# Attention on one Trainium2 core: TensorE takes the scores of two steps, then the P times V products of two earlier steps, by turns

## The reference

```python
x = x + _L0_conv_ref(_gn(x), w_qkv, w_proj, b_proj)          # attention over the 1024 pixels, 8 heads of 48
x = x + _L1_conv_ref(_gn(x), proj_w, proj_b, off_w, off_b, mask_w, mask_b, gamma, beta)   # deformable 3x3 convolution, batch norm, GELU
```

```python
attn = jnp.einsum('bhnd,bhmd->bhnm', q, k) * SCALE
attn = jax.nn.softmax(attn, axis=-1)
out = jnp.einsum('bhnm,bhmd->bhnd', attn, v)
```

## Time and profile before

| | |
|---|---|
| time before, median of 3 runs | 3718.53 us (3712.7 to 3722.61) |
| the profiled execution | 3713.13 us, its span 3711.2 us |
| TensorE matmuls busy | 3324.8 us (90%) |
| VectorE, ScalarE, GpSimd busy | 2285.5 (62%), 1694.9 (46%), 1278.6 us (34%) |
| TensorE clock granted, mean | 0.96 of full |
| the attention stage, batch 1 | 652.88 us to about 757 us |

### The profile page before, as it was taken

One profiled execution on the slowest core, in us unless ns is written; L12 is line 12 of the kernel. 1 busy time (PEld: TensorE's weight loads), 2 busy tenths in 40 slices (PEclk: granted clock), 3 DMA queues, 4 the chain that ended last, 5 costly groups with the idle time before them and its releaser, 6 DMA issues.

```text
span 3711.2 us, 88927 instructions
## 1 busy us (share of the span) xinstructions
PE 3324.8 (90%) x33434; PEld 1912.5 (52%) x33434; DVE 2285.5 (62%) x3746; ACT 1694.9 (46%) x2708; POOL 1278.6 (34%) x1183
## 2 busy tenths in 40 slices
PE   4799899989999899998999899998999989997991
PEld 1245555545555455554555455564555545554660
DVE  5576566755767567665676557675676756764343
ACT  3155443644436444454436444374444544454443
POOL 0043232622326133342335233271333523353440
PEclk8689999999999999999999999999999999998996
DMA  3000000100010000100001000100001000001007
GB/s 132 0 19 36 1 2 3 37 35 2 2 37 3 35 2 2 37 36 1 2 2 38 35 1 2 37 3 35 2 1 37 19 18 1 2 20 69 1 1 306
DMA packets 12151, 97.80 MB, mean 26 GB/s; under 512 B 2777, under 2 KB 2905, under 8 KB 4972
## 3 DMA queue, kind: packets, MB, share of 16 engines
q1 hardware_dynamic: 9468, 67.41, 4.7%
q0 software_dynamic: 1152, 12.58, 0.8%
q10 hardware_dynamic: 1008, 11.01, 0.8%
HBM read 56.26 MB, written 34.60 MB: 24 GB/s over the span
## 4 chain that ended last, share of the span: by engine, by line
PE 51%; issue 23%; POOL 15%; DVE 5%; ACT 4%; DMA 1%; DVEq 0%; POOLq 0%; SPq 0%; ACTq 0%
PE R L1513 20%; POOL PL L612 13%; PE R L1494 12%; PE G L1258 6%; PE G L1291 5%; PE G L1482 2%; DVE MXP L1010 2%; PE R L1406 2%; PE R L1331 1%; DVE M L1187 1%; ACT PL L849 1%; PE G L1474 1%; PE G L1433 1%; PE G L1428 1%; ACT P L786 1%
## 5 line engine op out<-in xcount | busy, mean ns | idle before, releaser
L1513 PE MATMUL R<-P,WALL 128*128 128x512 f16 x3888 | 980.5, 379 | 0.3 <-issue 0.3
L1010 DVE TENSOR_REDUCE MXP<-G 128x1 f32<-128x512 f32 x1024 | 693.7, 688 | 173.8 <-PE G L1291 165.8
L612 POOL TENSOR_TENSOR PL<-P 128x1024 f16<-128x1024 f32 x256 | 574.3, 2248 | 626.8 <-ACT P L769 624.7
L1494 PE MATMUL R<-MHL,XB 128*128 128x240 f16 (+14 forms) x7776 | 720.3, 235 | 2.5 <-DVE P L1208 2.5
L649 POOL TENSOR_TENSOR MHL<-M,MHL 128x280 f16<-128x280 f32 (+2 forms) x576 | 364.8, 636 | 852.7 <-ACT MHL L859 851.5
L769 ACT ACTIVATE P<-R 128x1024 f32<-128x1024 f32 x512 | 521.2, 1024 | 237.7 <-PE R L1331 230.9
L1494 PEld LDWEIGHTS R<-MHL,XB 128*128 128x128 f16 x7776 | 569.9, 98 | 103.7 <-DVE P L1208 2.8
L1513 PEld LDWEIGHTS R<-P,WALL 128*128 128x128 f16 x3888 | 378.7, 98 | 395.1 <-issue 0.5
L1060 DVE TENSOR_TENSOR PL<-P 128x1024 f16<-128x1024 f32 x256 | 453.4, 1771 | 175.7 <-ACT P L769 175.5
L1331 PE MATMUL R<-QK 48*128 48x512 f16 (+1 forms) x3072 | 437.0, 393 | 53.2 <-issue 33.7
L1291 PE MATMUL G<-QK,QZ 112*128 112x512 f16 x1024 | 411.4, 403 | 45.2 <-DVE MXP L1010 17.1
(11 more groups left out here) (127 smaller groups left out, 3315.3 us busy)
## 6 DMA issues: line engine op xcount, KB each, us to landing
XA<-x SPq DMA_DIRECT2D x8, 1536.0 KB, 9.0
X<-x SPq DMA_DIRECT2D x8, 1536.0 KB, 6.5
x_scratch<-X SPq DMA_DIRECT2D x7, 1536.0 KB, 5.1
y_scratch<-XP ACTq DMA_DIRECT2D x7, 1536.0 KB, 7.6
WALL<-y_scratch SPq DMA_DIRECT2D x6, 1536.0 KB, 14.8
out<-WALL POOLq DMA_DIRECT2D x6, 1536.0 KB, 11.0
QK<-x_scratch SPq DMA_DIRECT2D x4, 1536.0 KB, 17.7
P<-wd SPq DMA_DIRECT2D x9, 576.0 KB, 4.7
```

The lines of the kernel that those rows point to most:

```text
L612: pool.tensor_tensor(PL[:, s % P_BUFS, :], P32[:, s % P_BUFS, :], high_view(s), ALU.subtract).then_inc(p_low_pool, 1)
L1010: dve.reduce_max(MXP[:, name[1] % 2, n // 2, n % 2:n % 2 + 1], chunk(sec, name)[:, :], AX.X).then_inc(dve_read, 1)
L1494: last = pe.matmul(out, XT[:, x_part, g * BOX_Y + r, t * 128:(t + 1) * 128], MHL[:, m_part, o + at:o + at + (hi - lo) * (x1 - x0)], start= ...
L1513: last = pe.matmul(R6[:, CT + ct, :], WALL[:, w:w + 128], PHL[:, u % 2, part // 2, t, :], start=(u % TAPS == 0 and n < CT), stop=(u % TAPS ...
```

## The change

TensorE's loop goes over two steps at a time. It issues both scores, then all that both steps had between them, then the two products that are 3 and 2 steps behind the even step. No instruction is added or removed, and the other engines' programs, their waits, the buffers and `LAG` stay as they are.

```diff
-                for s in range(STEPS + LAG):
+                for s in range(0, STEPS + LAG, 2):
                     if s < STEPS:
                         scores(s)
-                        for name in step_chunks(s, not final):
+                        scores(s + 1)
+                        for name in step_chunks(s, not final) + step_chunks(s + 1, not final):
                             if name[0] == "gn":
                                 group_mean(name, sec, b * 2 + 2)
                             else:
                                 fill_chunk(name, sec, b)
                     elif not final:
-                        fill_chunk(DRAIN[s - STEPS], sec, b + 1)
-                    if s >= LAG:
-                        pv(s - LAG)
+                        for name in DRAIN[s - STEPS:min(s - STEPS + 2, LAG)]:
+                            fill_chunk(name, sec, b + 1)
+                    for k in (s - LAG, s - LAG + 1):
+                        if 0 <= k < STEPS:
+                            pv(k)
                 if not final:
                     fill_chunk(DRAIN[LAG], sec, b + 1)
```

## The result

The changed kernel takes 3726.2 us (median of 14 runs, 3723.3 to 3730.2), the one before beside it 3716.45 (14 runs). The ratio is 1.0026, with a 95% interval of 1.0017 to 1.0034: slower by a quarter of a per cent, 9.8 us. Forecast was 3699, faster. The time lies in the stated range, but the direction is the wrong one. The profiled execution took 3723.3 us, 10.2 more than the one before.

What follows compares the result with a forecast made beforehand. TensorE's order of matmuls was taken as the bound. Seven batches at 6.3 - 3.3 - 1.0 = 2.0 and a last at 6.3 - 0.9 - 0.2 = 5.2 make 19.2 us less: 3699 from the median, range 3684 to 3737.

Steps and rivals of the forecast that it cites:

- The order: TensorE's two-step round: fewer changes between scores and pv make 2.93 into 2.72, saving 0.21, 6.3 us a batch.
- the loop: Odd exponential, its wait for pv(s - 3), scores and pv: 2.66 a round, 0.06 below 2.72, so not binding.
- the rival that made it the bound: Odd exponential's wait for pv(s - 3) longer than 0.83 makes ScalarE's loop the bound: slower, up to 3743; chance 0.14.
- The insertion: Two ScalarE operations between exponentials after steps 24, 32 and 40: 1.71 lost each time, in seven batches.
- the group mean: Group mean's share in the cost of ScalarE's other work: 0.23 a batch, in seven batches.
- the pair of low parts: VectorE's and GpSimd's low parts wait for each other: 2.84 a pair, falling behind by 0.12 a round.
- low part 20: Late at step 20, where VectorE waits for GpSimd's power behind low part 19: 0.9 of waiting, 1.0 a batch in all.
- Block normalising, o_norm and the readings: 0: These wait for things done over a microsecond earlier, so they cost 0.
- last batch, drift of the pair relieved by step 38: Low parts fall behind for 17 rounds x 0.12 less 1.1: 0.9 by step 38, where transposes relieve it.
- the first: Rival: VectorE and GpSimd's low parts set every round at 2.84; 3719, chance 0.15.
- The second and third: Rivals: ScalarE's loop becomes the bound, up to 3743, chance 0.14; change of shape isn't the cost, 3737, chance 0.08.
- The case "better": Nothing late on the low parts' side: 3.0 a batch, last 6.1, 3691; insertions also no dearer, 3669; chance 0.14.

Runs made afterwards that it cites:

- e12: e7 with 6 added matmuls nobody reads between the two scores in rounds 26, 34 and 42 of the first seven batches; single run, 3702.4 us.
- e7: Changed kernel with GpSimd's low part cut to 128 of 1024 columns, the rest of odd steps' low part left out; 3699.7 us, 0.9956.
- e2: Changed kernel with the transpose of step 61 moved to step 62; 3715.7 us, ratio 0.9989 to the kernel before.
- e10: Changed kernel with 6 added matmuls nobody reads between the two scores in rounds 26, 34 and 42 of the first seven batches; 3741.65 us, 1.0064.
- e3: Changed kernel with rounds 26, 34 and 42 of the first seven batches in TensorE's old order; 3711.8 us, 0.9987.
- e4: Changed kernel with the edits of e1, e2 and e3 together; 3705.5 us, ratio 0.9966 to the kernel before.
- e11: Changed kernel with ScalarE's insertions moved behind the exponentials of steps 25, 33 and 41; 3714.1 us, 0.9992.
- e6: Changed kernel with GpSimd's power ahead of low part 19, transpose at 62, old order in rounds 18, 20, 22, 26, 34, 42 except last batch; 3693.7 us, 0.9941.
- e1: Changed kernel with VectorE's group-norm shift (L975) ahead of the low part of step 22 instead of step 20; 3727.4 us, 1.0028.
- e5: Changed kernel with GpSimd's group-norm power computed ahead of low part 19 instead of behind it; 3708.5 us, 0.9983.
- e8: Kernel before with GpSimd's low part cut to 128 of 1024 columns, the rest of odd steps' low part left out; 3710.5 us, 0.9984.

## Why the prediction was wrong, point by point

**Right.** The order: six more scores at once, the shape changes saved, a round of 2.72. ScalarE's odd exponential waits for pv(s - 3), 0.87 behind its start where 0.83 was taken, and the loop doesn't bind: the rival that made it the bound needed 0.15 more than 0.83. The insertion costs 4.45 - 2.72 = 1.73 where 1.71 was worked out, the group mean 0.22 for 0.23. That the turns between scores and pv are the cost, and not a semaphore each, stands on the same 2.72. Whether it is the rows of the tiles or another thing in which the two differ (their types, their columns) was not tried. With low parts and falls away the whole working is there: 89.65 - 86.68 = 2.97 a batch (e12, forecast 3.0) and 6.14 in the last (forecast 6.1). And the pair of low parts at 2.84, which the last batch shows in 12 of its rounds.

**Wrong, with sizes.** From 19.2 faster to 10.2 slower, by the profiled executions, are 29.4 us (by the medians 29.0):

| step of the prediction | forecast | shown | us in all |
|---|---|---|---|
| the granted clock, in no term of the sum | 0 | falls in the stage 14.4, in the first five steps 2.6 | 17.0 |
| low part 20, "0.9 of waiting there" (1.0 a batch) | 1.0 | 6.79 - 4.46 (e7) = 2.33 | 9.3 |
| "Block normalising, o_norm and the readings: 0" | 0 | 0.72, 0.90 in the last | 5.9 |
| last batch, drift of the pair relieved by step 38 | 0.9 | 82.71 (e2) - 81.23 (e7) = 1.5 | 0.6 |
| all else, the most of it between the stages | | | -3.4 |

- *The clock.* The sum was made at the granted clock of 1.00 that the earlier trace rows shows, and costed each stall at its own length. The stalls that the change makes are followed by stretches at half clock. Counted from the intervals they cost 1.4 in the two rounds from step 33 in six of seven batches (8.5), 1.0 in three behind step 20 (3.1) and 1.4 twice in the first batch (2.8). e10, e12, e3, e4, e11 and e6 have none from step 33. From 700 us on in batch 1, TensorE's longest wait for an exponential is 0.2 us in e10 and e12, 0.9 in e3, e4 and e6, and 1.0 in e11: no fall from step 33 on in any of these six kernels' 42 batches. It is 1.6 in the changed kernel, e1, e2 and e5, and falls from step 33 on stand in 7, 7, 7 and 3 of their seven batches. e12 against e7 gives 17.6 for the falls in a kernel without low parts. The clock is the largest term and decided the sign: without its 17.0 the changed kernel would be 6.8 faster.
- *Low part 20.* The prediction named the queue behind the power, and gave L975, which is 0.16 in the earlier trace rows, no price of its own. L975 has two inputs in SBUF, and GpSimd's low part 21 had started 0.06 ahead of it. What GpSimd does next, right behind the power, was the part left out. e5 shows it: the power one place earlier, and 1.9 of the 2.15 are gone. The Trainium skill (SBUF — State Buffer, Who interferes with whom) says that issue order, not the shape of the operation, decides who blocks. L975 agrees: with one element a partition it takes 1.84 us instead of 0.16.
- *The transpose.* The claim was that all these readings wait for things done over a microsecond earlier. That holds for four of five: the round that takes two transposes costs 3.64 - 2.72 = 0.92, twice what one cost before (3.41 - 2.93 = 0.48). For step 61 no row was behind it: there L1072 of block 6 ends 0.66 after TensorE could take the transpose. e2 gives back exactly 0.72 and 0.90.
- *The last batch.* The mechanism was right; a slack of 1.1 was to last nine rounds and lasted about four: the round is 2.76 from step 11 and 2.83 from step 13. Twelve rounds x 0.11 and a little at both ends are 1.5, not 0.9.

(The prediction says of the round of 2.84 that it is "the second rival"; in its list it is the first.) Of the rivals, the first (a round of 2.84 everywhere) holds in the last batch alone. The second and third fell. The case "better" was the right account of the order itself, and the missing part was what its stalls cause. Batch 1's time without a matmul in the stage went from 1.8 us to 7.4, of which 4.6 for ScalarE, 2.2 for low part 20 and 0.7 for the transpose.

**Open.** What decides that a stall is followed by a fall. e5 has the same waits in seven batches and falls in three; the changed kernel and e2 differ only at step 61, and have the paid falls behind step 20 in different batches. That TensorE idled ahead of the falls is shown, and that filling one idle takes the fall away at that place (e10, e12). Open too is the start of a batch, which moved by 3 us in e10 and e12 and by 1 in e6.

## What to carry to other kernels

When an order closes gaps inside an engine's steady round, write down what the gaps paid for: here the slack that absorbed ScalarE's insertions and a late low part, so that 0.21 a round was paid for with four times the idle time (1.8 us a batch to 7.4). Cost such a stall at its length and again at the clock that may follow it, and use the tight order only in rounds where nobody is far behind: e6_where, with the power moved ahead and one transpose a step later, gained 20 us where the order in all rounds lost 10. Before saying that moving a wait made it dearer or cheaper, look at the granted clock of both stretches: in e1 and e4 the difference was a fall. For an engine whose operation waits for another's result, look also at what that other engine issues right behind the result.

## What the runs showed of the hardware

- The granted clock of TensorE fell from 1.00 to 0.50 (1.2 GHz) for some 3.4 us, about 1 us after the end of an idle of 1.53 us in a stage otherwise full of matmuls, with TensorE busy again when it fell. In e5 the same idle times had no such sequel in four of seven batches. One fall costs 1.37 us (e7 against e12), and nothing where idle time that was there anyway takes it up (changed kernel, batch 2, step 24).
- Going from scores (49 rows, in tiles) to pv (128 rows) and back costs about 0.21 us: 29 rounds gave 6.14 in the last batch, e7 against e8.
- A VectorE operation of one element a partition took 0.16 us alone and 1.84 when it started 0.06 behind a low part of GpSimd.
- GpSimd's small power took 0.54 with VectorE idle and 1.50 to 1.53 beside a low part of VectorE.
